# Experts stage of a two-layer network: router scores of 2048 tokens as wide products in four column strips, turned by four products, and partial sums added on GpSimd

## The reference, cut to what matters

```python
def _L1_ffn_ref(x, router_w, router_b, expert_w, expert_b):   # K = 2
    router_probs = softmax(x @ router_w + router_b)
    top_p, top_i = top_k(router_probs, K)
    top_p = top_p / sum(top_p)
    expert_out = einsum('bnd,edc->bnec', x, expert_w) + expert_b      # 8 experts
    gathered = take_along_axis(expert_out, top_i[..., None], axis=2)
    return einsum('bnk,bnkc->bnc', top_p, gathered)

x = x + _L1_conv_ref(_ln_c(x), ...)
t = _to_tokens(x)
t = t + _L1_ffn_ref(_ln_t(t), router_w, router_b, expert_w, expert_b)
```

## Time and profile before

| | |
|---|---|
| median of 3 runs | 3136.38 us (3129.91 to 3153.72) |
| the profiled execution | 3149.02 us, its span 3147.3 us |
| mean granted TensorE clock, share of full | 0.899 |
| TensorE busy | 2528.9 us (80%) |
| VectorE busy | 1538.8 us (49%) |
| ScalarE busy | 1355.0 us (43%) |
| GpSimd busy | 258.7 us (8%) |
| experts' products, first to last start | 2656.37 to 3143.71 us |

### The profile page before, as it was taken

How to read it: one execution, slowest core, us unless ns; L and a number is a source line. 1 busy time by engine, 2 the same in 40 slices (tenths; PEclk the granted TensorE clock), 3 DMA queues, 4 the chain that set the end, 5 groups by cost and what they waited for, 6 DMA issues and landing times. The chain is left out here.

```text
span 3147.3 us, 88222 instructions
## 1 busy us (share of the span) xinstructions
PE 2528.9 (80%) x36744; PEld 1963.3 (62%) x36744; DVE 1538.8 (49%) x3563; ACT 1355.0 (43%) x2712; POOL 258.7 (8%) x477
## 2 busy tenths in 40 slices
PE   0565999545429999999999999999796884999999
PEld 0334888522128888888888888888633751555555
DVE  6441344233506565656565656565411343466666
ACT  0562344155016565656565656566410354232332
POOL 0102112000010000000000000000012001101000
PEclk9866899677859999999999999999998776799999
DMA  6437556422451111111111111110178520000000
GB/s 201 124 97 121 106 106 115 117 119 102 128 138 45 41 41 41 41 41 41 41 41 42 41 41 41 41 41 21 51 265 285 176 61 12 9 22 19 22 17 27
DMA packets 189043, 242.48 MB, mean 77 GB/s; under 512 B 36891, under 2 KB 147278, under 8 KB 185146
## 3 DMA queue, kind: packets, MB, share of 16 engines
q1 hardware_dynamic: 154325, 124.05, 14.7%
q0 software_dynamic: 30368, 94.52, 11.1%
q10 hardware_dynamic: 3969, 18.31, 1.5%
HBM read 145.54 MB, written 91.27 MB: 75 GB/s over the span
## 5 line engine op out<-in xcount | busy, mean ns | idle before, releaser
L962 DVE COPY spc_g<-spc_pz 128x512 f32<-128x512 f32 x1088 | 670.8, 683 | 446.8 <-PE spc_pz L860 446.7
L940 ACT ACTIVATE spc_g<-spc_pz 128x512 f32<-128x512 f32 x1088 | 587.2, 612 | 345.6 <-PE spc_pz L860 343.7
L860 PE MATMUL spc_pz<-spc_v,spc_as 108*128 108x128 bf16 x8704 | 599.9, 222 | 38.6 <-issue 27.7
L860 PEld LDWEIGHTS spc_pz<-spc_v,spc_as 108*128 108x128 bf16 x8704 | 515.2, 99 | 132.8 <-issue 46.0
L878 PE MATMUL spc_pz<-spc_g,spc_u 128*20 128x128 f32 x17408 | 503.7, 274 | 31.7 <-DVE spc_g L962 18.2
L878 PEld LDWEIGHTS spc_pz<-spc_g,spc_u 128*20 128x20 f32 x17408 | 480.0, 134 | 64.6 <-ACT spc_g L940 41.3
L1602 DVE SCALAR_TENSOR_TENSOR moe_yt<-moe_ex,moe_gb,moe_yt 128x128 f32<-128x128 f32 x768 | 209.6, 344 | 146.7 <-ACT moe_yt L1506 145.7
L845 PE MATMUL spc_pu<-spc_f,spc_s 128*128 128x256 f32 x816 | 222.6, 399 | 71.8 <-DMA spc_s<-s_sf 71.8
L1456 PE MATMUL moe_ex<-moe_ew,moe_d 128*128 128x512 f32 x512 | 254.0, 619 | 16.8 <-DVE moe_yt L1602 16.8
L507 DVE SCALAR_TENSOR_TENSOR inv_xo<-inv_pa,inv_mask,inv_xo 128x256 f32<-128x256 f32 x256 | 123.6, 484 | 222.7 <-PE inv_pa L465 163.9
L485 ACT ACTIVATE inv_b<-inv_pb 112x1024 f32<-112x1024 f32 x128 | 125.2, 1021 | 221.1 <-PE inv_pb L444 221.1
(11 more groups left out here) (195 smaller groups left out, 2407.6 us busy)
## 6 DMA issues: line engine op xcount, KB each, us to landing
s_yd<-spc_yo SPq DMA_DIRECT2D x136, 160.0 KB
spc_s<-s_sf POOLq DMA_DIRECT2D x36, 512.0 KB, 6.4
...
```

What stands on the lines that cost most here:

```text
L860: m = pe.matmul(pz[:, (p + 2) % 3, e // 4, 2 * FT * (e % 4):2 * FT * (e % 4) + 2 * FT], AS[:, x, 8 * p + e, :], V[:, k, x, :, FT * t:FT * ...
L940: act.activation(g_out(p, 0), g_in(p, 0), ACT.Copy).then_inc(ga, 1)
L962: v.tensor_copy(g_out(p, 1), g_in(p, 1)).then_inc(gd, 1)
```

## The change

The scores of a group are no longer made tile by tile. With all four chunks' `d` and `sq` ready, four products with the padded weights `rw` (32 columns, of which 8 are used) stream 512 tokens each and write to four strips of 32 partitions of `pd`; four more with `onec` (32 columns, of which the ninth is 1/128) add the variance to the same strips. ScalarE copies the bank to `lt`, and four products of 128 x 128 turn it into `pl`, tokens on the partitions. That happens at tiles 8 and 9. The views `logits` and `variance` read `pl` with strides.

GpSimd adds the two partial sums of each tile in place, and `final` has two products instead of three; it waits for `summed`. GpSimd's neighbour loads for the group after the next stand behind its sums of tiles 4 to 12. Constants are set and loaded in another order, and in two earlier stages a semaphore `passed`, which nobody waits for, is gone.

```diff
--- before.py
+++ after.py
@@ -237,7 +237,6 @@
         nm_ready, xn_ready, xn_turned = A.sem("nm_ready"), A.sem("xn_ready"), A.sem("xn_turned")
         xnc_ready, eps_ready = A.sem("xnc_ready"), A.sem("eps_ready")
         reduced, red_ready = A.sem("reduced"), A.sem("red_ready")
-        passed = A.sem("passed")
         block = A.ctx.enter_context(nc.Block())
         xv = I["x"].rearrange("b c (n m) -> b n c m", m=CH)
 
@@ -331,7 +330,6 @@
                     m.then_inc(st_ready, 1)
                 for k in range(D):
                     v.wait_ge(st_ready, D * i + k + 1)
-                    v.sem_inc(passed, 1)
                     for t in range(NT):
                         m = v.bn_aggr(mv[:, k, t, :], st[:, k, t, :])
                     m.then_inc(mv_ready, 1)
@@ -1335,11 +1331,11 @@
     NGR, GC, GT = NB * T // GR, GR // CH, GR // P
     NTILE = NGR * GT
     NM = NE - 2
-    LW = GT * NE + GT
     with Arena(nc, "moe") as A:
         ident, cmat, eps = A.sb("ident", [P, P]), A.sb("cmat", [P, P]), A.sb("eps", [P, 1])
-        onec = A.sb("onec", [P, 1])
-        ew, rw = A.sb("ew", [P, NE * C]), A.sb("rw", [P, NE])
+        ew = A.sb("ew", [P, NE * C])
+        rw, onec = A.sb("rw", [P, 32]), A.sb("onec", [P, 32])
+        lt = A.sb("lt", [P, CH])
         rb, prio = A.sb("rb", [P, NE]), A.sb("prio", [P, NE])
         eb = A.sb("eb", [P, GT, C])
         v9 = A.sb("v9", [9, 2, 32, W])
@@ -1358,28 +1354,29 @@
         const_in, set_up = A.sem("const_in"), A.sem("set_up")
         v9_in = [A.sem(f"v9_in{k}") for k in range(2)]
         conv_done, x3_ready, d_done = A.sem("conv_done"), A.sem("x3_ready"), A.sem("d_done")
-        d_ready, sq_ready, lv_done = A.sem("d_ready"), A.sem("sq_ready"), A.sem("lv_done")
+        sq_ready, lv_done = A.sem("sq_ready"), A.sem("lv_done")
+        score_done, lt_ready = A.sem("score_done"), A.sem("lt_ready")
         r_step, arg_ready, exp_ready = A.sem("r_step"), A.sem("arg_ready"), A.sem("exp_ready")
         gate_ready, gt_turned, gt_ready = A.sem("gate_ready"), A.sem("gt_turned"), A.sem("gt_ready")
         chain, ex_done, begun = A.sem("chain"), A.sem("ex_done"), A.sem("begun")
         mixed, yt_used, fin_ready = A.sem("mixed"), A.sem("yt_used"), A.sem("fin_ready")
+        summed = A.sem("summed")
         outs = [A.sem(f"outs{k}") for k in range(2)]
         block = A.ctx.enter_context(nc.Block())
 
-        def logits(i):
-            return pl[:, LW * (i % 2):LW * (i % 2) + GT * NE]
-
-        def variance(i):
-            return pl[:, LW * (i % 2) + GT * NE:LW * (i % 2) + LW]
-
-        gt_at = pl[:, 2 * LW:2 * LW + P]
+        lv = pl[:].rearrange("p (k c m) -> p c k m", k=4, c=GC)
+        logits, variance = lv[:, :, :, 0:NE], lv[:, :, :, NE]
+        gt_at = pl[:, 0:P]
+
+        def by_chunk(a):
+            return a.rearrange("p (c k) e -> p c k e", c=GC)
 
         @block.sync
         def _(sp):
-            for dst, src in ((ident[:], I["ident"]), (cmat[:], I["cmat"]), (ew[:], I["expert_w"]), (rw[:], I["router_w"]),
-                             (rb[:], I["router_b"].partition_broadcast(P)), (prio[:], I["prio8"])):
+            for dst, src in ((ident[:], I["ident"]), (cmat[:], I["cmat"]), (ew[:], I["expert_w"]), (rb[:], I["router_b"].partition_broadcast(P)), (prio[:], I["prio8"])):
                 sp.dma_start(dst, src).then_inc(const_in, 16)
-            sp.wait_ge(set_up, 3)
+            sp.wait_ge(set_up, 5)
+            sp.dma_start(rw[:, 0:NE], I["router_w"]).then_inc(const_in, 16)
             for t in range(GT):
                 sp.dma_start(eb[NE * t:NE * t + NE, t, :], I["expert_b"]).then_inc(const_in, 16)
             dst = out.rearrange("b c (n m) -> b n c m", m=CH)
@@ -1392,17 +1389,30 @@
         @block.gpsimd
         def _(pool):
             pool.memset(eb[:], 0.0).then_inc(set_up, 1)
-            pool.memset(onec[:], 1.0 / C).then_inc(set_up, 1)
+            pool.memset(rw[:], 0.0).then_inc(set_up, 1)
             pool.memset(eps[:], EPS_T).then_inc(set_up, 1)
+            pool.memset(onec[:], 0.0).then_inc(set_up, 1)
+            pool.wait_ge(set_up, 4)
+            pool.memset(onec[:, NE:NE + 1], 1.0 / C).then_inc(set_up, 1)
             rows = S["VP"].rearrange("h b w -> b h w")
-            for i in range(NGR):
-                if i >= 2:
-                    pool.wait_ge(conv_done, GC * (i - 1))
-                for ti in range(3):
-                    for tj in range(3):
-                        r0 = (i % 2) * 32 + ti
-                        pool.dma_start(v9[3 * ti + tj:3 * ti + tj + 1, i % 2],
-                                       rows[i // 2:i // 2 + 1, r0:r0 + 32, tj:tj + W]).then_inc(v9_in[i % 2], 16)
+
+            def neighbour(i, tap):
+                ti, tj = divmod(tap, 3)
+                r0 = (i % 2) * 32 + ti
+                pool.dma_start(v9[tap:tap + 1, i % 2],
+                               rows[i // 2:i // 2 + 1, r0:r0 + 32, tj:tj + W]).then_inc(v9_in[i % 2], 16)
+
+            for i in range(2):
+                for tap in range(9):
+                    neighbour(i, tap)
+            for idx in range(NTILE):
+                i, t = divmod(idx, GT)
+                pool.wait_ge(mixed, NM * idx + NM)
+                pool.tensor_tensor(yt[:, idx % 3, 0], yt[:, idx % 3, 0], yt[:, idx % 3, 1], ALU.add).then_inc(summed, 1)
+                if i + 2 < NGR and 4 <= t < 13:
+                    if t == 4:
+                        pool.wait_ge(conv_done, GC * (i + 1))
+                    neighbour(i + 2, t - 4)
 
         @block.tensor
         def _(pe):
@@ -1418,15 +1428,20 @@
                 pe.wait_ge(x3_ready, GC * i + c + 1)
                 pe.matmul(pd[:], cmat[:], x3[:, i % 2, c], start=True, stop=True).then_inc(d_done, 1)
 
-            def scores(i, c):
-                if c == 0 and i:
+            def scores(i):
+                pe.wait_ge(sq_ready, GC * i + GC)
+                for c in range(GC):
+                    pe.matmul(pd[32 * c:32 * c + 32, :], rw[:], d[:, i % 2, c], start=True, stop=False, skip_group_check=True)
+                for c in range(GC):
+                    m = pe.matmul(pd[32 * c:32 * c + 32, :], onec[:], sq[:, c], start=False, stop=True, skip_group_check=True)
+                m.then_inc(score_done, 1)
+
+            def turn_scores(i):
+                if i:
                     pe.wait_ge(gt_ready, i)
-                pe.wait_ge(d_ready, GC * i + c + 1)
-                pe.wait_ge(sq_ready, GC * i + c + 1)
-                for t in range(GC * c, GC * c + GC):
-                    o = P * (t % 4)
-                    pe.matmul(logits(i)[:, NE * t:NE * t + NE], d[:, i % 2, c, o:o + P], rw[:], start=True, stop=True)
-                    m = pe.matmul(variance(i)[:, t:t + 1], sq[:, c, o:o + P], onec[:], start=True, stop=True)
+                pe.wait_ge(lt_ready, i + 1)
+                for k in range(4):
+                    m = pe.transpose(pl[:, P * k:P * k + P], lt[:, P * k:P * k + P], ident[:])
                 m.then_inc(lv_done, 1)
 
             def final(idx):
@@ -1435,19 +1450,18 @@
                     pe.wait_ge(gt_ready, i + 1)
                 if t % 4 == 0 and idx >= 8:
                     pe.wait_ge(fin_ready, idx // 4 - 1)
-                pe.wait_ge(mixed, NM * idx + NM)
+                pe.wait_ge(summed, idx + 1)
                 o = pf[:, idx // 4 % 2, P * (t % 4):P * (t % 4) + P]
                 pe.matmul(o, yt[:, idx % 3, 0], ident[:], start=True, stop=False)
-                pe.matmul(o, yt[:, idx % 3, 1], ident[:], start=False, stop=False)
                 pe.matmul(o, eb[:, t], gt[:, i % 2], start=False, stop=True).then_inc(yt_used, 1)
 
             pe.wait_ge(const_in, 16 * (6 + GT))
-            pe.wait_ge(set_up, 3)
+            pe.wait_ge(set_up, 5)
             for c in range(GC):
                 conv(0, c)
                 centre(0, c)
-            for c in range(GC):
-                scores(0, c)
+            scores(0)
+            turn_scores(0)
             for idx in range(NTILE):
                 i, t = divmod(idx, GT)
                 if idx >= 2:
@@ -1466,8 +1480,10 @@
                         conv(i + 1, t // 2)
                     if t < 2 * GC and t % 2 == 1:
                         centre(i + 1, t // 2)
-                    if 3 <= t < 2 * GC + 3 and t % 2 == 1:
-                        scores(i + 1, t // 2 - 1)
+                    if t == 2 * GC:
+                        scores(i + 1)
+                    if t == 2 * GC + 1:
+                        turn_scores(i + 1)
             final(NTILE - 2)
             final(NTILE - 1)
 
@@ -1476,13 +1492,19 @@
             def centred(i, c):
                 act.wait_ge(d_done, GC * i + c + 1)
                 if i >= 1:
-                    act.wait_ge(lv_done, GC * (i - 1) + c + 1)
-                act.activation(d[:, i % 2, c], pd[:], ACT.Copy).then_inc(d_ready, 1)
+                    act.wait_ge(score_done, i)
+                act.activation(d[:, i % 2, c], pd[:], ACT.Copy)
```

(19 more changed lines are left out.)

## The result

The changed kernel takes **3097.90 us** (median of 4 runs, 3093.47 to 3112.50) against 3134.82 us of the kernel before beside it (4 runs, 3129.91 to 3153.72): ratio 0.9855, 95% interval 0.9820 to 0.9891. A later comparison with more runs gave 0.9895 (0.9861 to 0.9930). Ratios here leave out runs more than 1.5% above the fastest of their kernel and are not plain quotients of the two medians (0.9882 in the first comparison, which lies in its interval). In both the kernel is faster by more than the scatter and by less than 2%: the medians differ by 37 and 33 us, where 40 us were forecast.

What follows compares the result with a forecast made beforehand. TensorE bounds only 35.47 of a group's 57.05 us (tiles 0 to 9), then ScalarE 6.62 and VectorE 14.96. Savings 47.5, less contention 3.5 and clock 4, give 40 us: 3136.4 - 40 = 3096 us, range 3082 to 3120.

Steps and rivals of the forecast that it cites:

- Removed and added products: TensorE-bound tiles 0 to 9 of a group: scores -5.1, finals -2.0, strips +1.9 us, from 35.47 to 30.27 us.
- rival 3: Score strips do not overlap: 6.9 instead of 1.9 us in 7 groups, 10 more at the start; 3141 us; chance 0.05.
- ScalarE part: Group stretch after tile 9, before tile 10: Ln's 0.36 us wait goes, two table loads remain; 6.62 to 6.27 us.
- GpSimd's add: Sum of a tile's two partial sums on GpSimd, 128 columns: 0.4 us, taken from 0.2 to 0.6.
- The free time before TensorE waits: Before a tile's final products: GpSimd has about 1.7 us free, behind the product of the tile two later.
- Rival 4: Slow GpSimd sum: TensorE waits over 1.8 us, GpSimd sets the pace from 3.3; at 3.8, 3200 us; chance 0.03.
- Contention: VectorE-bound part: GpSimd's sum delays VectorE's gate steps, 0.5 us a group, 3.5 over seven boundaries.
- Rival 1: VectorE and GpSimd shut each other out in every step: 21 us instead of 3.5, 3114 us; chance 0.13.
- Start and group 0: Half-clock start of the experts saves 6.7 us; group 0, with seven finals, saves 5.1 before contention.
- Last group: Its 14 tiles go from 2.39 to 2.17 us, saving 2.8; the GpSimd hand-over before the last finals adds 0.4.
- Clock: Longer TensorE gap before tile 0, about 1.9 us, drops the clock at two or three of seven boundaries: 4 us lost.
- Edits in two earlier stages cost nothing: Stages ahead of the experts: removing a semaphore nobody waits for costs nothing.

Runs made afterwards that it cites:

- early load: Changed kernel with the Ln table loaded at tile 8 by a one-column Ln: 3102.36 us, ratio to before 0.9849; again 3112.28 us, 0.9905.
- four adds: Changed kernel with three more same-size GpSimd additions, results unused, ahead of each sum: 3127.17 us, 1 run.
- six adds: Changed kernel with five more same-size GpSimd additions, results unused, ahead of each sum: 3132.63 us, 1 run.
- the kernel before alone: Kernel before with only the semaphore `passed` taken out of two earlier stages: 3142.80 us, ratio to before 0.9994.

## Why the prediction was right

- **Removed and added products: right.** Tiles 0 to 9 take 30.05 us (30.27 forecast): three scores and nine finals gone, strips 1.86 us. Apart, the strips saved 3.41 us there (3.2 forecast) and the finals 2.01 (2.0). That the four strips run side by side, and rival 3 does not hold, is shown by 1.07 us for four of them.
- **ScalarE part: right.** 6.18 us (6.27). The early load showed that it is the table loads that set it.
- **GpSimd's add: a little mis-sized.** 0.453 us for 0.4, which was a choice out of 0.2 to 0.6: the memset row gave 0.88 ns a column, and the adds measured here cost 2.1 ns a column (272 ns for 128 more). The free time before TensorE waits was there: with four adds its products waited once in a group, 0.2 us. Rival 4 needed 3.3 us a tile and is far off: with 2.7 us a group still was 54.0 to 54.6, under 57.05. In the last group, with its shorter tiles, GpSimd with six adds set the pace, at 2.6 us a tile already, which the rival's 3.3 did not allow for.
- **Contention: the size was off, the mechanism right.** 0.33 us a group for 0.5, from two steps of 0.29 that took 0.45. Rival 1 (every step, products too) is out. The Trainium skill (SBUF — State Buffer, "Who interferes with whom") says that a VectorE instruction with two SBUF inputs contends with GpSimd's reads, that one with at most one SBUF input (two-port modes aside) does not, and that the shared ports are an exclusive lock. The trace agrees: the stretched steps end 0.14 to 0.16 us behind the adds, and the reductions stay at 286 ns.
- **Start and group 0: right, the second within its scatter.** 6.7 us (6.7), and 5.4 (5.1 less 0.5). From turning to turning group 0 took 62.12 and 61.37 us in the two profiles before and 56.72 and 55.32 after, with the clock at 0.50 for 6 to 9 us of it; agreement closer than 1 us is luck here.
- **Last group: wrong by 1.8 us.** "+0.4" for the end was +0.3 in the products, but SyncE's closing wait grew by 2.2 us, which I had not priced.
- **Clock: wrong for this kernel, by the whole 4 us.** "I expect a fall at two or three of the seven boundaries: 4 us." The gap in front of tile 0 grew to 1.66 us, once 1.80 (1.9 forecast), and the granted clock was 1.00 behind each of the seven, for instance:

```profile
2743.50:2745.50 2.00, 1.76 (x4) 0.87 (x5) 1.79 (x8) 0.00 (x0) 0.45 (x1) 1.00 0.00 0
...
3052.80:3054.80 2.00, 1.84 (x5) 0.89 (x6) 1.79 (x8) 0.00 (x0) 0.45 (x1) 1.00 0.00 0
```

The idle spot of the earlier trace rows was shorter (1.47 us) and was followed by 0.50. With four adds a gap of 1.76 us was followed by 0.50 at two boundaries and by 1.00 at four, so the length of one gap does not decide. That kernel did what was forecast for this one: three falls, at 1.15 us each. So the mechanism exists, in a kernel whose gap is 0.1 us longer and whose VectorE part is 1.1 us longer; which of the two brings it on is not shown.
- **"Edits in two earlier stages cost nothing": right in the kernel before alone (0.9994), not settled in the changed one.** There 14 us of the stage's 47 did not reach the time in the later comparison (3 to 25 by its interval), with a clock that was lower ahead of the experts.
- **The time itself: near by luck.** 3096 was forecast and 3097.9 measured. But the stage saved 45.6 us, 5.6 more than the 40 forecast, from the 4 us for the clock, 2.5 in the six full groups and 0.8 in group 0, less 1.8 in the last. The two medians gave only 36.9 of it, and medians of four runs can be some 10 us off.
